# A fused attention and mixture-of-experts block: own lag for every operation, score groups of four lanes, causal mask by GpSimd selects

## The chip, the cores and the metric

The kernel runs on one core of one Trainium2 chip. The metric is the device time of one execution in microseconds (us), as the median of several runs. The core has five engines that each work through a queue of their own, in order: TensorE (PE; its weight loads are listed as PEld), VectorE (DVE), ScalarE (ACT), GpSimd (POOL) and SyncE (SP, here only for DMA). They wait for each other by semaphores.

## The reference

Input x is 8 batches of 256 rows of 128 numbers, all float32. Each batch is normalised (`xn`), and two branches of `xn` are added to x.

```python
x = L0_attn_x
xn = _layernorm(x, axis=-1)
x = x + attn(xn) + ffn(xn)
# attn: qkv = xn @ w_qkv.T; one head, no mask
att = softmax(q @ k.T * 128**-0.5)
y = einsum('bqk,bvd->bqd', att, v) @ w_fc.T + b_fc
return layernorm(xn + y) * gamma + beta
# ffn: 16 heads of 8, causal
h = rms(x, n1_w)
q, k, v = rms(heads(wq), qn_w), rms(heads(wk), kn_w), heads(wv)
scores = where(causal, q @ k.T * 8**-0.5, -inf)
ao = softmax(scores) @ v @ wo.T      # first 32 columns set to 0
x = x + ao
xf = rms(x, n2_w)
wts = top 2 of softmax(xf @ gate_w.T), normalised, over 4 experts
return x + sum(wts[e] * expert_e(xf))   # first 32 columns of the sum are 0
```

The experts are small stacks of 128x256 and 256x256 layers with gelu or silu: `e0` (up, down), `e1` (w1, w2, down, silu by tanh), `e2` (l1, l2, l3, l4), `e3` (down, up, out).

## The kernel before

A batch of 256 rows is two tiles of 128. The work on one batch is cut into four stages, and one slot of the software pipeline works on four batches at a time: L (layer norm, turning `xn`, the projections), A (norm of Q and K by three Newton steps on VectorE, their transposes), B (causal attention, the other attention branch, the output projection, the residual and `xf`) and C (gate and experts). `stages` gives slot t the batches L = t, A = t - 1, B = t - 2, C = t - 3, so 8 batches take 11 slots, t = 0 to 10. All operations of a stage have the same lag. Each engine has a function `slot` in which the order of its operations within a slot is written out by hand, and waits name the exact event that is needed. PSUM has four shared banks (`a`, `pv`, `even`, `odd`), each filled and read in the fixed cyclic order of `BANK_FILLS`, and a four-bank tile `scores_ps`.

Causal attention: the 16 heads stand in 4 lanes of 32 partitions and 4 groups. A matmul of one lane uses 32 rows of the array (`tile_position=(32*lane, 0)`), so lanes can lie side by side in it. `scores(u)` (line 1174) computes one unit, half a group, two lanes: for each lane 256 queries by the first 128 keys and 128 queries by the other 128 keys. There are 8 units for each batch, 64 in all. To each unit's scores TensorE adds the mask (line 1186): a bf16 matmul of the identity with `later_keys`, which holds -1e30 where the key comes after the query. ScalarE's `exp_unit` (line 463) writes exp of a unit to `probs`, unmasked parts and masked ones (which become 0) alike. `weigh_v(g)` (lines 1203 and 1207) multiplies by V with four lanes in four column tiles, and fills bank `pv`; VectorE turns the result (`pv_turn`, line 769). A unit waits only for the exp of the unit two before it, so that two units alternate. A second program, with a search of row maxima (`find_maxima`), runs only if the weights of the norms are large; on these inputs it does not run.

Further names: `x_turn` and `qk_turn` (line 1111) transpose on TensorE; `qkv_project` (1143), `q0_project` (1136), `a0_scores` (1216), `fc_row` (1224); `wo_project` (1232), `xf_turn`, `gate` (1251); `up_layer` (1266) for E1A, E1B, L1, D3, E0; `square_layer` (1278) for L2, L3; `e3_up_layer` (1288) for U3; `down` (1304). ScalarE evacuates with gelu (line 524), tanh (508), copies (484, 491, 500, 536, 538), squares (548). ScalarE has tables for its functions: the order of `slot` puts all exps and the tanh of a slot first and all gelus behind, so a full slot has two switches of table, ACT_TABLE_LOAD. VectorE's pairs of 128x128 operations are `ln_normalise` (975), `h0_norm` (903) and `residual_scale` (945). GpSimd has small powers and 128x256 additions (lines 301 to 417).

```python
# the order of slot on TensorE, one line for each stretch
scores(0); scores(1); a0_scores(0); scores(2); up E1A; scores(3)
a0_scores(1); weigh_v(0); scores(4); up E1B; scores(5); weigh_v(1)
fc_row(); scores(6); scores(7); weigh_v(2); up L1; weigh_v(3); up D3
qk_turn(); L2; U3; L3; wo_project(); up E0
x_turn(); qkv_project(0); down(0); xf_turn(); qkv_project(1)
down(1); q0_project(); gate()
```

Of the kernel before, what the change touches and what calls it, by code (L numbers as in the profile page):

```python
# [1 line left out]

# [2 lines left out]

ALU = mybir.AluOpType
ACT = mybir.ActivationFunctionType
F32 = mybir.dt.float32
F32R = mybir.dt.float32r
# [4 lines left out]
P = 128  # L14
FLOAT_MAX = 3.4028234663852886e38
# [12 lines left out]
}  # L28


def fill_ordinals(slots):

    table = {bank: {} for bank in BANK_FILLS}
    for slot in slots:
        for bank, fills in BANK_FILLS.items():
            for fill, stage in fills:
                if slot[stage] is not None:
                    table[bank][fill, slot[stage]] = len(table[bank])
    return table


def fused_block(nc: bass.Bass, x, cols, rows, w_proj, w_first, w_up, w_mid, w_down, out):
# [14 lines left out]
    with ExitStack() as ctx:  # L57
# [6 lines left out]
        def sem(name):  # L64
# [4 lines left out]
        pv_ps, a_ps = psum("pv_ps"), psum("a_ps")  # L69
        even_ps, odd_ps = psum("even_ps"), psum("odd_ps")  # L70
# [41 lines left out]
        xn = [sb(f"xn{r}", [P, TILES, D]) for r in range(3)]  # L112
# [49 lines left out]
                   ln_stats ln_scaled xn_ready a_full a_read qk_ready v_ready  # L162
                   scores_full exp_done pv_full pv_read
                   a0_maxed a0_rowed xsum_ready h0_stats h0_scaled h0_normed ao_ready
                   xnb_ready x1_started x1_squared x1_scaled xf_ready acc_ready
                   gate_shifted gate_exped e1_tanh
                   even_full even_read odd_full odd_read
                   dve_a dve_b dve_c dve_d dve_l dve_s pool_l pool_b pool_s""".split()
        s = {n: sem(n) for n in names}
# [3 lines left out]
        DVE_A, DVE_B, DVE_C, DVE_D, POOL_L, POOL_B = 14, 4, 15, 6, 5, 3  # L173
# [3 lines left out]
        def stages(t):  # L177
            numbers = {"L": t, "A": t - 1, "B": t - 2, "C": t - 3}
            return {stage: n if 0 <= n < BATCHES else None for stage, n in numbers.items()}

        SLOTS = [stages(t) for t in range(BATCHES + 3)]
        at = fill_ordinals(SLOTS)

        block = ctx.enter_context(nc.Block())

        def wait(eng, name, value):

            if not isinstance(value, int) or value > 0:
                eng.wait_ge(s[name] if isinstance(name, str) else name, value)

        def fill_free(eng, bank, fill, batch):

            wait(eng, f"{bank}_read", at[bank][fill, batch])

        def fill_ready(eng, bank, fill, batch):

            wait(eng, f"{bank}_full", at[bank][fill, batch] + 1)

        def fill_emptied(eng, bank, fill, batch):

            if batch >= 0:
                wait(eng, f"{bank}_read", at[bank][fill, batch] + 1)

        def pipeline(slot):
            for t in range(1, len(SLOTS)):
                slot(**SLOTS[t])


        @block.sync
        def _(sp):  # L210
            sp.dma_start(x_sb[0][:], x[0].rearrange("(j p) d -> p j d", p=P)).then_inc(x_in[0], 16)
            sp.dma_start(proj[:], w_proj).then_inc(s["proj_in"], 16)
            sp.dma_start(first[:], w_first).then_inc(s["first_in"], 16)
            sp.dma_start(x_sb[1][:], x[1].rearrange("(j p) d -> p j d", p=P)).then_inc(x_in[1], 16)
# [4 lines left out]
            def rows_of(t, batch):  # L219
                return t[batch].rearrange("(j p) d -> p j d", p=P)  # L220

            def slot(L, A, B, C):
                if L is not None and L >= 2:
                    wait(sp, "xn_ready", L - 1)
                    sp.dma_start(x_sb[L % 2][:], rows_of(x, L)).then_inc(x_in[L % 2], 16)
                if B is not None:
                    wait(sp, out_done[B % 2], 16 * (B // 2))
                    sp.dma_start(acc[B % 2][:], rows_of(x, B)).then_inc(acc_in[B % 2], 16)
                if C is not None:
                    fill_emptied(sp, "even", "DN0", C)  # L230
                    fill_emptied(sp, "odd", "DN1", C)
                    sp.dma_start(rows_of(out, C), acc[C % 2][:]).then_inc(out_done[C % 2], 16)

            slot(**SLOTS[0])
            pipeline(slot)
# [5 lines left out]
        def _(pool):  # L241
            def step(ins, name, value):

                ins.then_inc(s[name], 1)
                pool.wait_ge(s[name], value)

            step(nc.gpsimd.memset(ident[:], 0.0), "pool_s", 1)
# [4 lines left out]
            def constants():  # L252

                step(nc.gpsimd.memset(lane_rows[:], 1.0), "pool_s", 2)
# [28 lines left out]
                pool.wait_ge(s["zeros_ready"], 2)  # L283

            def slot(L, A, B, C):
                l, a, b = L, A, B
                k = {"pool_l": POOL_L * l if L is not None else 0, "pool_b": POOL_B * b if B is not None else 0}

                def step_of(ins, name):
# [1137 lines left out]
```

## Time and profile before

| what | us |
|---|---|
| median of 3 runs | 306.5 (302.14 to 308.01) |
| the profiled execution | 302.12 |
| its span, first to last instruction | 300.4 |
| TensorE busy | 261.5 |
| ScalarE, VectorE, GpSimd busy | 151.1, 144.5, 73.0 |

The profile is of one execution on the chip. Its page gives the busy time of each engine, the chain of work that ended last, and groups of instructions by line; each further view is an answer of the same trace. Busy time counts overlapping instructions of an engine once. The ends of matmuls are modelled, and spans on GpSimd are rough. Lines such as L1174 are lines of the kernel before.

### The profile page before, as it was taken

What the parts mean: (1) busy time and instruction counts of PE and PEld (TensorE: products, weight loads), DVE (VectorE), ACT (ScalarE), POOL (GpSimd) and SP (SyncE); (2) the same over time, 40 slices, a digit from 0 to 9 for tenths busy, and PEclk for the clock granted to TensorE, in tenths of its full rate; (3) what the DMA queues carried; (4) which work ended last, traced back from release to release, by engine and by line L of the source; (5) the groups of instructions that cost most, each with busy time, mean ns of one, the idle gap of its engine ahead of it and who ended that gap; (6) DMA issues with size and microseconds to landing.
All of it is one profiled execution on the core that took longest, in us unless ns stands there. A gap on an engine that the chain in (4) does not pass through costs nothing.

```text
span 300.4 us, 5450 instructions
## 1 busy us (share of the span) xinstructions
PE 261.5 (87%) x1940; PEld 187.3 (62%) x1940; DVE 144.5 (48%) x608; ACT 151.1 (50%) x298; POOL 73.0 (24%) x163
## 2 busy tenths in 40 slices
PE   0717997599998999899989998999899989998784
PEld 0302654166687667776777676866686678667564
DVE  2360345115742585349522962387248525452713
ACT  1222344334564656556665657556656564654530
POOL 4731301440042223214240515050610052006000
PEclk9999999557999999999999999999999999999999
DMA  7510000000000100010001000010001000000000
GB/s 194 211 39 2 1 0 2 2 0 2 0 0 2 53 2 0 2 52 3 0 3 41 14 0 1 25 30 2 0 3 37 2 0 20 17 2 0 21 0 17
DMA packets 7567, 6.05 MB, mean 20 GB/s; under 512 B 624, under 2 KB 7024, under 8 KB 7536
## 3 DMA queue, kind: packets, MB, share of 16 engines
q1 hardware_dynamic: 7248, 5.44, 5.7%
q10 hardware_dynamic: 288, 0.21, 0.5%
q8 instruction: 18, 0.29, 0.4%
q14 instruction: 13, 0.11, 0.1%
HBM read 4.60 MB, written 1.05 MB: 19 GB/s over the span
## 4 chain that ended last, share of the span: by engine, by line
PE 78%; DVE 6%; DMA 4%; ACT 4%; issue 3%; POOL 1%; SPq 1%; ACTq 0%; DVEq 0%; POOLq 0%
PE scores_ps L1174 17%; PE even_ps L1278 9%; PE scores_ps L1186 6%; PE odd_ps L1266 6%; PE pv_ps L1203 6%; PE a_ps L1143 5%; PE even_ps L1304 5%; PE odd_ps L1304 5%; PE even_ps L1266 4%; PE a_ps L1216 3%; DMA x_sb<-in_x 3%; PE odd_ps L1288 2%; PE pv_ps L1207 2%; PE a_ps L1111 2%; DMA first<-in_first 2%
## 5 line engine op out<-in xcount | busy, mean ns | idle before, releaser
L463 ACT ACTIVATE probs<-scores_ps 128x768 f32<-128x768 f32 x64 | 51.7, 808 | 44.0 <-PE scores_ps L1186 44.0
L1174 PE MATMUL scores_ps<-qT,kT 32*128 32x256 f32 (+1 forms) x512 | 64.4, 373 | 0.0
L1174 PEld LDWEIGHTS scores_ps<-qT,kT 32*128 32x128 f32 x512 | 47.5, 200 | 20.0 <-issue 14.9
L1278 PE MATMUL even_ps<-l_h,mid 128*128 128x256 f32 x128 | 31.0, 385 | 0.0
L327 POOL TENSOR_SCALAR h_rstd<-h_mv 128x2 f32<-128x2 f32 x8 | 1.5, 192 | 113.1 <-DVE h_mv L893 113.1
L1186 PE MATMUL scores_ps<-later_keys,ident_bf 128*128 128x256 bf16 x128 | 26.6, 292 | 0.0
L1143 PE MATMUL a_ps<-qkvT,xnT 128*128 128x384 f32 x32 | 18.4, 663 | 9.4 <-ACT xnT L484 8.0
L1278 PEld LDWEIGHTS even_ps<-l_h,mid 128*128 128x128 f32 x128 | 23.2, 190 | 4.4 <-ACT l_h L524 1.8
L1266 PE MATMUL odd_ps<-xfT,up 128*128 128x256 f32 x80 | 22.3, 394 | 2.3 <-DVE e_h L761 1.7
L769 DVE STREAM_TRANSPOSE pv_rows<-pv_ps 128x256 f32<-128x256 f32 x32 | 14.3, 446 | 19.3 <-PE pv_ps L1207 19.3
L524 ACT ACTIVATE l_h<-even_ps 128x512 f32<-128x512 f32 x24 | 14.6, 607 | 15.9 <-PE even_ps L1278 15.8
L1203 PE MATMUL pv_ps<-probs,v_aug 128*32 128x256 f32 x256 | 20.9, 399 | 0.6 <-DVE pv_rows L769 0.6
L844 DVE TENSOR_REDUCE a_negmax<-a_ps 128x1 f32<-128x256 f32 x16 | 6.6, 414 | 30.3 <-PE a_ps L1216 30.3
L991 DVE SCALAR_TENSOR_TENSOR acc<-even_ps,wts,acc 128x96 f32<-128x96 f32 x32 | 10.2, 318 | 17.5 <-issue 8.5
L1266 PE MATMUL even_ps<-xfT,up 128*128 128x256 f32 x64 | 18.2, 410 | 0.2 <-DVE e_s L752 0.2
L387 POOL TENSOR_SCALAR ln_tmp<-ln_mv 128x2 f32<-128x2 f32 x8 | 2.0, 249 | 63.0 <-DVE ln_mv L964 50.7
L500 ACT ACTIVATE qkv<-a_ps,h_scale 128x384 f32<-128x384 f32 x16 | 9.3, 580 | 15.4 <-PE a_ps L1143 15.4
L945 DVE TENSOR_SCALAR xf<-x_sb,x_scale 128x128 f32<-128x128 f32 x16 | 8.5, 569 | 17.8 <-POOL x_scale L371 17.8
L1266 PEld LDWEIGHTS odd_ps<-xfT,up 128*128 128x128 f32 x80 | 13.4, 190 | 5.4 <-DVE e_h L761 2.1
L1143 PEld LDWEIGHTS a_ps<-qkvT,xnT 128*128 128x128 f32 x32 | 6.1, 236 | 14.1 <-ACT xnT L484 10.4
L473 ACT ACTIVATE a_exp<-a_ps,a_negmax 128x256 f32<-128x256 f32 x16 | 7.6, 474 | 11.6 <-DVE a_negmax L844 11.2
L1266 PEld LDWEIGHTS even_ps<-xfT,up 128*128 128x128 f32 x64 | 11.4, 199 | 3.1 <-issue 1.4
(151 smaller groups left out, 473.7 us busy)
## 6 DMA issues: line engine op xcount, KB each, us to landing
x_sb<-in_x SPq DMA_DIRECT2D x8, 128.0 KB, 2.5
acc<-in_x SPq DMA_DIRECT2D x8, 128.0 KB, 2.1
out<-acc SPq DMA_DIRECT2D x8, 128.0 KB, 1.9
mid<-in_mid SPq DMA_DIRECT2D x1, 640.0 KB, 7.3
up<-in_up SPq DMA_DIRECT2D x1, 578.0 KB, 6.2
downs<-in_down SPq DMA_DIRECT2D x1, 512.0 KB, 8.1
first<-in_first SPq DMA_DIRECT2D x1, 320.0 KB, 5.3
row<-in_rows ACTq DMA_DIRECT2D x1, 200.0 KB, 4.8
```

The lines of the kernel that those rows point to most:

```text
L463: nc.scalar.activation(probs[g % 2][:, 2 * half:2 * half + 2, 0:SEQ + P], scores_ps[:, 2 * half:2 * half + 2, 0:SEQ + P], ACT.Exp).then_in ...
L500: nc.scalar.activation(qkv[:, j, :], a_ps[:, 0:3 * D], ACT.Copy, scale=h_scale[:, j:j + 1]).then_inc(s["a_read"], 1)
L524: nc.scalar.activation(flat, ps[:, 0:ncol], ACT.Gelu).then_inc(s[f"{bank}_read"], 1)
L769: V.transpose(pv_rows[:, g].rearrange("p n e -> p (n e)"), pv_ps[:, 0:SEQ]).then_inc(s["pv_read"], 1)
L991: ins = V.scalar_tensor_tensor(out=rows, in0=(even_ps, odd_ps)[j][:, e * KEPT:(e + 1) * KEPT], scalar=wts[:, j, e:e + 1], in1=rows, op0=AL ...
L1143: T.matmul(a_ps[:, 0:3 * D], xnT[L % 2][:, j * P:(j + 1) * P], qkvT[:], start=True, stop=True).then_inc(s["a_full"], 1)
L1174: ins = T.matmul(ps, kT[p][rows, g, kt * P:(kt + 1) * P], qT[p][rows, kt * P:SEQ], start=kt == 0, stop=False, tile_position=(32 * lane, 0))
L1186: ins = T.matmul(own, ident_bf[:], later_keys[:].unsqueeze(1).to_broadcast([P, TILES, P]), start=False, stop=True)
L1203: T.matmul(rows[:, 0:SEQ], v_aug[p][:, 0, GROUPS * lane + g, :], pr[:, lane, 0:SEQ], start=True, stop=False, tile_position=(0, 32 * lane))
L1266: ins = T.matmul(ps[:, m * SEQ:(m + 1) * SEQ], wT[:, m * P:(m + 1) * P], xfT[C % 2][:], start=True, stop=True)
L1278: ins = T.matmul(even_ps[:, m * SEQ:(m + 1) * SEQ], wT[:, at:at + P], src[:, ci, :], start=(ci == 0), stop=(ci == HC - 1))
L1304: ins = T.matmul(ps[:, e * KEPT:(e + 1) * KEPT], hidden[e][:, ci, j * P:(j + 1) * P], downs[:, e, ci, MASKED:], start=(ci == 0), stop=(ci ...
```

## The change

- Stages are gone. Each operation takes its batch number from the slot with a lag of its own, from 0 to 4, and has a new place in `slot` on its engine. Groups 0 of scores and exps of a batch come one slot before groups 1 to 3; `down` on TensorE comes one slot later than the other expert layers. There are 12 slots, t = 0 to 11.
- The order of the fills of each bank changes with it, and the head (first batch's turn and projections) is written ahead of the slots.
- `scores(n, g)` issues one group, all four lanes, and waits for both exps of the group before.
- The mask matmuls are dropped in the program that runs here. After each exp, GpSimd's `mask(n, u)` sets the part of `probs` with keys behind the query to 0 by an `affine_select` over 128x512 elements, 8 for each batch. `weigh_v` waits for the selects, not for the exps.
- ScalarE's order puts exps between the gelus: L1, E0, L2, D3, then exps of units 0 and 1, then L3, U3, then exps of units 2 and 3.
- Several waits become explicit (what a buffer's reader has done); the two programs remain, with the mask matmuls kept in the one that searches for maxima.

```diff
-    "a": (("S00", "B"), ("S01", "B"), ("FC", "B"), ("QKT", "A"), ("XT", "L"), ("QKV0", "L"), ("QKV1", "L"), ("Q0T", "L")),
+    "a": (("QKV1", 1), ("Q0T", 1), ("S00", 2), ("S01", 2), ("FC", 2), ("QKT", 1), ("XT", 0), ("QKV0", 0)),
...
+            def mask(n, u):
...
+                g, half = divmod(u, HALVES)
+                pool.wait_ge(s["exp_done"], UNITS * n + u + 1)
+                own = probs[g % 2][:, 2 * half:2 * half + 2, :].rearrange("p l (n q) -> p (l n) q", q=SEQ)[:, :, 0:P]
+                nc.gpsimd.affine_select(out=own, in_=own, compare_op=ALU.is_ge, fill=0.0, base=0,
+                                        pattern=[[0, 2 * TILES], [1, P]], channel_multiplier=-1
+                                        ).then_inc(s["masked"], 1)
...
-                    wait(pe, "exp_done", UNITS * b + u - 1)
+                wait(pe, "exp_done", UNITS * n + HALVES * g)
...
-                        for lane in (2 * half, 2 * half + 1):
+                    for lane in range(LANES):
...
-                    wait(pe, "exp_done", UNITS * b + HALVES * (g + 1))
+                wait(pe, "masked", UNITS * n + HALVES * (g + 1))
```

The new orders, as the kernel after has them (lag behind the name):

```python
# TensorE
qkv(1) 1; scores(1) 2; weigh_v(0) 2; q0 1; down(0) 4; down(1) 4; a0_scores(0) 2
xf_turn 3; scores(2) 2; gate 3; E1A 3; a0_scores(1) 2; weigh_v(1) 2
scores(3) 2; E1B 3; fc_row 2; weigh_v(2) 2; L1 3; E0 3; qk_turn 1; L2 3; D3 3
weigh_v(3) 2; x_turn 0; scores(0) 1; qkv(0) 0; L3 3; U3 3; wo 2
# ScalarE
exp 4, 5 of 2; tanh 3; a0_softmax(1) 2; gate_exp 3; exp 6, 7 of 2
gelu L1 3; gelu E0 3; q_copy, k_copy x4 1; gelu L2 3; gelu D3 3; x_copy 0
exp 0 of 1; qkv_copy(0) 0; exp 1 of 1; gelu L3 3; qkv_copy(1) 0; gelu U3 3
x1_square x2 2; exp 2 of 1; q0_copy 0; exp 3 of 1; xf_copy 2; a0_softmax(0) 1
# GpSimd
h0_gamma 3; mask 3 of 2; v_copy 1; h0_beta 3; h0_add 3; mask 4 to 7 of 2
ln x4 0; x1_add 3; h_eps, h_pow 0; biased 1; h0_variance 2; x1_start 2
h0_scale 2; mask 0, 1 of 1; x1_variance, x1_pow 2; mask 2 of 1
```

## Rows read from the trace of the kernel before

**Rows 1.** Page, part 1: busy us (share of the span), instructions

```profile
PE 261.5 (87%) x1940; PEld 187.3 (62%) x1940; DVE 144.5 (48%) x608; ACT 151.1 (50%) x298; POOL 73.0 (24%) x163
```

**Rows 2.** Table by stretch, one full slot: us, length, busy of each engine, clock, DMA

```profile
129.00:160.26 31.26, 29.96 (x243) 22.25 (x242) 17.26 (x75) 18.50 (x38) 8.49 (x17) 1.00 0.05 14
```

**Rows 3.** Chain in order of time, slots at full clock: start us, us, what

```profile
181.27 1.82 PE even_ps L1278 x8
...
186.66 1.76 PE even_ps L1304 x16
...
188.63 0.65 PE a_ps L1143 x2
...
191.84 0.85 PE scores_ps L1174 x8
192.69 0.32 PE scores_ps L1186 x2
...
198.56 0.57 PE pv_ps L1203 x8
199.13 0.22 PE pv_ps L1207 x8
```

**Rows 4.** Page, part 5: group, count, busy us, mean ns, idle before

```profile
L1174 PE MATMUL scores_ps<-qT,kT 32*128 32x256 f32 (+1 forms) x512 | 64.4, 373 | 0.0
L1186 PE MATMUL scores_ps<-later_keys,ident_bf 128*128 128x256 bf16 x128 | 26.6, 292 | 0.0
```

**Rows 5.** Chain in order of time, first 32 us

```profile
16.60 0.59 DVE xn L975 x2
...
19.86 1.10 PE a_ps L1111 x4
...
29.99 1.58 PE scores_ps L1174 x8
```

**Rows 6.** Table by stretch, between the first two attention slots

```profile
50.00:55.00 5.00, 2.34 (x9) 1.70 (x8) 2.26 (x9) 3.01 (x11) 2.45 (x5) 0.64 0.00 0
55.00:60.00 5.00, 2.98 (x6) 0.82 (x4) 0.93 (x2) 1.29 (x3) 2.19 (x4) 0.50 0.01 3
...
65.00:70.00 5.00, 5.00 (x24) 3.42 (x21) 2.53 (x11) 2.09 (x5) 1.93 (x5) 0.50 0.00 0
```

**Rows 7.** Chain in order of time, last 20 us

```profile
280.34 0.98 PE even_ps L1266 x4
...
292.76 2.00 PE even_ps L1304 x16
...
297.70 0.32 DVE acc L991
```

**Rows 8.** Groups by shape, GpSimd

```profile
L357 POOL TENSOR_TENSOR acc<-h0n,acc 128x256 f32<-128x256 f32 x8 | 5.8, 728 | 1.5 <-POOL h0n L349 0.5
...
L277 POOL TENSOR_SCALAR_AFFINE_SELECT mask_f<-mask_f 128x128 f32<-128x128 f32 x2 | 0.6, 298 | 0.3
...
L255 POOL TENSOR_SCALAR_AFFINE_SELECT lane_rows<-lane_rows 128x16 f32<-128x16 f32 x1 | 0.2, 230 | 0.1
```

**Rows 9.** Timeline of weight loads: start us, us, engine, line, tiles, count

```profile
191.77 0.19 PEld L1174 LDWEIGHTS scores_ps<-qT,kT 32*128 32x128 f32 x2
...
198.49 0.16 PEld L1203 LDWEIGHTS pv_ps<-probs,v_aug 128*32 128x32 f32 x8 [0.33 <-issue]
```

**Rows 10.** Timeline of ScalarE at a switch from exp to gelu

```profile
175.01 0.81 ACT L463 ACTIVATE probs<-scores_ps 128x768 f32<-128x768 f32 x1 [0.37 <-PE scores_ps L1186]
175.84 1.28 ACT L524 ACT_TABLE_LOAD   x1
177.14 0.60 ACT L524 ACTIVATE l_h<-even_ps 128x512 f32<-128x512 f32 x1
```

**Rows 11.** Timeline of VectorE and GpSimd, a pair alone and a pair beside GpSimd

```profile
180.24 0.60 DVE L903 TENSOR_SCALAR h0n<-h,h_mv,h_rstd 128x128 f32<-128x128 f32 x2 [0.73 <-POOL h_rstd L334]
...
185.87 0.72 POOL L379 TENSOR_TENSOR acc<-acc,x_sb 128x256 f32<-128x256 f32 x1
...
185.94 0.94 DVE L945 TENSOR_SCALAR xf<-x_sb,x_scale 128x128 f32<-128x128 f32 x2 [2.04 <-POOL x_scale L371]
```

More of the change, by code:

```diff
@@ L14 @@
 P = 128
+XN_COPIES = 3
+SLOTS_AFTER = 4
 FLOAT_MAX = 3.4028234663852886e38
@@ L23, with fill_ordinals, filled @@
 BANK_FILLS = {
[4 rows of a table removed]
-}
[L31 to L38, printed above, removed]
[4 rows of a table added]
+}
+HEAD_FILLS = ("XT", "QKV0", "QKV1", "Q0T")
+BANK_OF = {fill: bank for bank, fills in BANK_FILLS.items() for fill, _ in fills}
+def fill_ordinals(batches, slots):
+    table, count = {}, dict.fromkeys(BANK_FILLS, 0)
+    def filled(fill, batch):
+        if 0 <= batch < batches and (fill, batch) not in table:
+            table[fill, batch] = count[BANK_OF[fill]]
+            count[BANK_OF[fill]] += 1
+    for fill in HEAD_FILLS:
+        filled(fill, 0)
+    for t in range(slots):
+        for fills in BANK_FILLS.values():
+            for fill, lag in fills:
+                filled(fill, t - lag)
     return table
@@ L189, in wait, with fill_free @@
                 eng.wait_ge(s[name] if isinstance(name, str) else name, value)
[L191 to L206, printed above, removed]
+        def fill_free(eng, fill, n):
+            wait(eng, read_sem(fill), at[fill, n])
@@ L217, in _, with load_x, load_acc, store @@
             sp.dma_start(downs[:].rearrange("p e c d -> p (e c d)"), w_down).then_inc(s["down_in"], 16)
[L219 to L235, printed above, removed]
+            def load_x(n):
+                if not 2 <= n < BATCHES:
+                    return
+                wait(sp, "xn_ready", n - 1)
+                sp.dma_start(x_sb[n % 2][:], rows_of(x, n)).then_inc(x_in[n % 2], 16)
+            def load_acc(n):
+                if not live(n):
+                    return
+                wait(sp, out_done[n % 2], 16 * (n // 2))
+                sp.dma_start(acc[n % 2][:], rows_of(x, n)).then_inc(acc_in[n % 2], 16)
+            def store(n):
+                if not live(n):
+                    return
+                fill_emptied(sp, "DN0", n)
+                fill_emptied(sp, "DN1", n)
+                sp.dma_start(rows_of(out, n), acc[n % 2][:]).then_inc(out_done[n % 2], 16)
+            for t in range(BATCHES + 3):
+                load_x(t)
+                load_acc(t - 2)
+                store(t - 3)
             for p in range(2):
@@ L586, in _ @@
-            slot(**SLOTS[0])
-            pipeline(slot)
+            nc.scalar.copy(vfc[:], scores_ps[:, 1, 0:D]).then_inc(s["vfc_ready"], 1)
+            ahead = 1
+            for t in range(SLOTS):
+                slot(t)
         @block.vector
@@ L1184, in scores @@
-                    for lane in (2 * half, 2 * half + 1):
+                            T.matmul(ps, head_rows[rows, g:g + 1].to_broadcast([32, P]), negT[p][rows, kt * P:SEQ],
+                                     start=False, stop=False, tile_position=(32 * lane, 0))
+                    for lane in range(LANES):
                         own = scores_ps[:, lane, :].rearrange("p (n q) -> p n q", q=SEQ)[:, :, 0:P]
@@ new lines, in down @@
+            def down(n, j):
+                if not live(n):
+                    return
+                fill = f"DN{j}"
+                fill_free(pe, fill, n)
+                for done in ("E0", "E1B", "L3", "U3"):
+                    fill_emptied(pe, done, n)
+                if n == 0:
+                    pe.wait_ge(s["down_in"], 16)
+                for e in range(EXPERTS):
+                    for ci in range(HC):
+                        ins = T.matmul(ps_of(fill)[:, e * KEPT:(e + 1) * KEPT], hidden[e][:, ci, j * P:(j + 1) * P],
+                                       downs[:, e, ci, MASKED:], start=(ci == 0), stop=(ci == HC - 1))
+                ins.then_inc(full_sem(fill), 1)
```

1895 lines of the change are left out of this document (974 added, 921 removed), and 6 rows, old and new, of the table BANK_FILLS.

## The prediction, written before the change was run

> **What bounds the kernel now.** I read four views in this order. The page's first part: TensorE is busy for 261.5 of 300.4 us, no other engine for more than half [rows 1]. The table by slot (a slot is one turn of the software pipeline): a full slot takes 31.26 us, with TensorE busy for 29.96, ScalarE 18.50, VectorE 17.26 and GpSimd 8.49 [rows 2]. So in a full slot TensorE idles 1.3 us: its instructions set the pace, and only what leaves its queue counts. The chain in order of time says what fills it: a scores unit (two lanes) takes 0.85 us of tiled matmuls, then 0.32 of mask matmuls over the whole array; PV, with four lanes of the same two widths, takes 0.57 + 0.22 = 0.79 in all [rows 3]. The groups give the totals: 64.4 us for the scores, 26.6 for the masks [rows 4]. Last the ends: attention begins at 29.99, the first full slot ran largely at the lower level of TensorE's clock, and the last slot is a lone chain [rows 5 to 7].
>
> **The masks leave TensorE.** 64 units lose their mask: 26.6 us [rows 4], 8 x 0.32 = 2.6 a slot. GpSimd gets 64 selects of 128x512. No row has that size. Selects of 128x16 take 0.23 and of 128x128 0.30 [rows 8], a slope of 0.6 to 0.7 ns an element, so 0.57 us as the estimate; the nearest dearer row, two inputs of 128x256 in 0.73, scaled to 512 gives 1.45 as upper end; the lower end is 0.30. I take 0.57 (same operation): 4.6 us a slot, GpSimd at 13 of some 26, hidden. But each PV group now waits for exp and then select. Queued behind a waiting select are v_copy, the h0 and x1 chains and the layer norm of the next batch, for which VectorE and then the TensorE transposes wait. At least 2.4 us of other TensorE work lies between a scores group and the PV that needs it, except across a slot's start, so I charge nothing; without that cover it is 0.6 to 1.5 a group.
>
> **Four lanes together.** The first two weight loads of a unit, one for each lane, lie in the same 0.19 us, and in PV all eight weight loads lie within 0.16 us [rows 9]. So row-tiled lanes do run side by side, and 0.85 is the time of one lane's stream and not of two. For four I take 0.85 a group (PV's row, 0.79, is nearest below); if only two run at a time it is 1.70. A full slot falls from 8 x 0.85 = 6.8 to 4 x 0.85 = 3.4, over the run 27 us. What it costs: before, two units alternate, one read by ScalarE while TensorE fills the other; now a group waits until both exps (2 x 0.81) of the last one have read it.
>
> **TensorE's slot** becomes 29.96 - 2.6 - 3.4 = 24.0 us.
>
> **ScalarE gets two more table switches.** Its queue now goes exp, gelu (L1, E0, L2, D3), exp (0, 1), gelu (L3, U3), exp: four switches a slot for two. One costs 1.28 between an exp that ends at 175.82 and a gelu at 177.14, 1.32 in all [rows 10]: + 2.6, ScalarE at 21.1 of 24. The Trainium skill ("ScalarE: Activation LUTs", What ACT_TABLE_LOAD costs) puts a drain of about 1.38 us beside the load, 2.66 for every switch. By that rule four switches would be 10.6 a slot and ScalarE at 26.6, an estimate from that page which would make it the bound. The row leaves no room for a drain there, and the sum goes by the row.
>
> The tightest ring I find runs from the end of scores group 0 to the start of group 2. ScalarE: load 1.3, exp 0.8, qkv copy 0.6, exp 0.8, load 1.3, gelu 0.6, qkv copy 0.6, gelu 0.6, two squares 1.0, load 1.3, exp 0.8, q0 copy 0.4, exp 0.8 = 10.9. TensorE by its chain: two qkv 1.3, L3 1.82, group 1 0.85, PV 0.79, two downs 3.52 [rows 3], and five shorter pieces of 0.22 to 0.86 in the same answer (U3, WO, q0, a0 and the xf transpose), 2.4 together = 10.7. ScalarE's times are those of its groups in the page. So it misses by 0.2. I charge 1.7 us of waits a slot: 1.3 as now, 0.4 for this. Full slot: 24.0 + 1.7 = 25.7.
>
> **Own lags: head.** VectorE's Newton chain loses the 0.6 of the second batch's xn in its middle, so the Q and K transposes start at 19.2 for 19.86 and K is copied by 22.1. The scores of batch 0 no longer queue behind the second batch's projections: they start near 22.8 for 29.99 [rows 5]. There a unit takes 1.58 for 0.85, the lower level of TensorE's clock by its duration. Slot 2's queue at twice the times of rows 3: four groups 6.8, two qkv 3.3, the copy between them 0.6, two PV 2.4, q0 1.2, two a0 1.7, a wait for the softmax 0.9 = 16.9, to 39.7. The rest (fc 0.42, two PV 1.6, transposes 0.66, K's copies 1.2, group 0.85, qkv 0.65, WO 0.42) is 5.8 at the upper level, which TensorE now reaches at 40, and 11 at the lower: slot 3 starts at 45.5 to 51. I take 47, for 62.27 now. Before, TensorE was busy for only 5.3 of the 10 us from 50 to 60, and the granted clock was 0.50 from 55 to 70 [rows 6]; scores units turn to 0.85 only after 71.2, so in 62.27 to 71.2 some 4.5 us are the clock's. The new queue has other work in that gap; I count slot 3 at the upper level, and keep 4.5 for the range.
>
> **Own lags: tail.** One slot more, as the downs are a slot later. Slot 10: downs of batch 6, 3.5, then the last batch's layers, 280.34 to 292.76 now = 12.4, with E0 moved into its gaps, 12.1: 15.6. Slot 11: downs 3.6, VectorE 1.35, store 2.4 = 7.3 [rows 7].
>
> **Sum.** Slot 3 at 47.0; slot 3 without downs 22.2; slots 4 to 7, 4 x 25.7 = 102.8; slot 8 without a new batch 24.8; slot 9, without its first steps (3.3), 22.4; slots 10 and 11 15.6 + 7.3. Span 242.1, from 300.4. The profiled execution took 302.1, 1.7 more than its span: 243.8. The median of the runs shown, 306.5, lies 1.4% above that execution, so I forecast 247 us.
>
> **VectorE and GpSimd.** The same pair of 128x128 VectorE operations takes 0.60 with GpSimd idle and 0.94 while GpSimd adds acc from 185.87 to 186.59 [rows 11]. So GpSimd's reads stop VectorE, and eight selects a slot are eight more such meetings. The Trainium skill ("SBUF — State Buffer", SBUF: two separate sides) says that such an operation and GpSimd's take their common port in turns and the loser fully blocks. By that rule, which the row bears out, the selects could hold VectorE for 8 x 0.57 = 4.6 a slot: 21.9 of 25.7, still below TensorE, but its chains (newton, down, residual) get later. It is a rival.
>
> **The rivals.**
> - *Pairs only* (0.12). Four lanes at once contend, two run at a time: 32 x 0.85 = 27 more, 274. For it: nothing in rows 9 shows four loads of 128 columns together. Against it: the pair's loads overlap fully.
> - *ScalarE's ring sets the slot* (0.12). Its 21.1 busy us can't be packed; both added loads become TensorE waits before the scores: 2.6 x 7.5 slots = 20, 267. For it: the ring above is short by 0.2. Against it: before, scores waited little.
> - *Selects block VectorE* (0.08). Half of the 4.6 us a slot comes through: 8 x 2.3 = 18, 265; all of it, 283.
> - *Slower than before* (0.04): the single hand-over. If the queues never get ahead, TensorE stands before every group for both exps, before PV for a select, and for both added loads: 6.5 + 2.3 + 2.6 = 11.4 a slot, 86 us in 7.5 slots, 333. It decides from 7.5 us of new waits a slot; the saving is 7 a slot with the ends. Against it: 2.4 to 8 us of independent work between groups, and ScalarE has 3 us free.
> - That the change does not do what it says is the first of these; the masks can't stay, as nothing issues them.
>
> **Chances.** Forecast 0.60 (own range 237 to 257: waits of 0.5 to 3 a slot), the rivals as given, 0.02 for less than 235, 0.02 for a hand-over that eats just the gain. The range 232 to 276 holds the lower bounds (groups at 0.79 save 2, no waits at all 13) and the first three rivals; the slow one is left out. A measurement of this kernel tells about 2% from no change: faster by over 2% 0.94, within 0.02, slower 0.04.
>
> **What would show it.** Scores groups of sixteen passes in about 0.85 and none of the mask matmuls: TensorE busy near 205 us. About 31 table loads for 16. Selects near 0.57. First scores near 23, slots of 25 to 26 us, second stretch of low clock gone or short. TensorE waits on exp or on the selects of over 3 us a slot would make the ring or the hand-over right; groups of 1.7 the first rival; VectorE busy over 165 us with the pairs of 0.94 common, the third.

## The result and the profile after

| | before | after |
|---|---|---|
| median, 4 runs each on one chip | 305.75 (302.14 to 308.01) | 236.34 (234.24 to 238.25) |
| profiled execution, its span | 302.12, 300.4 | 236.41, 234.6 |

The ratio is 0.774 (95%: 0.763 to 0.785). Some executions of a kernel take 1.5 to 5% longer than its fastest, and the ratios in this text are worked out without these. The forecast was 247 with a range of 232 to 276: the sign and the range held, the size was 10.7 us too high. The narrower range of 237 to 257, to which the prediction gave its chance of 0.60, was missed by 0.7 us on its low side.

The page of the kernel after, part 1 and three groups of part 5 (before: [rows 1, 4]):

```profile
PE 206.7 (88%) x1812; PEld 156.0 (67%) x1812; DVE 160.5 (68%) x608; ACT 160.3 (68%) x310; POOL 114.1 (49%) x227
...
L324 POOL TENSOR_SCALAR_AFFINE_SELECT probs<-probs 128x512 f32<-128x512 f32 x64 | 40.9, 639 | 48.5 <-ACT probs L506 47.0
...
L1241 PE MATMUL scores_ps<-qT,kT 32*128 32x128 f32 (+1 forms) x512 | 31.4, 361 | 0.3
...
L568 ACT ACT_TABLE_LOAD x14 | 18.0, 1283 | 0.3
```

TensorE has 128 instructions fewer, and the same 512 scores passes take 31.4 us for 64.4. The table by slot (us, length, busy of PE, PEld, DVE, ACT, POOL, granted clock, DMA share, GB/s), from slot 3 to the end:

```profile
43.92:69.39 25.47, 22.84 (x195) 16.51 (x196) 19.40 (x65) 18.48 (x37) 14.76 (x28) 0.93 0.01 2
93.53:117.67 24.14, 24.14 (x227) 18.99 (x227) 19.59 (x75) 20.40 (x40) 13.48 (x25) 1.00 0.06 18
165.93:189.06 23.13, 23.13 (x227) 18.33 (x225) 18.61 (x69) 20.04 (x38) 11.46 (x19) 1.00 0.05 13
189.06:210.24 21.18, 20.82 (x198) 16.56 (x199) 13.20 (x56) 14.11 (x27) 8.64 (x15) 1.00 0.05 14
210.24:227.01 16.77, 13.90 (x77) 11.05 (x77) 8.39 (x38) 7.80 (x15) 3.80 (x6) 1.00 0.03 8
227.01:234.60 7.59, 3.78 (x32) 3.62 (x32) 2.54 (x8) 0.00 (x0) 0.00 (x0) 0.88 0.07 21
```

The second row stands for slots 4 to 7. The reader is to see two equal numbers in it: 24.14 us long, 24.14 busy. TensorE doesn't stop at all; before it was 31.26 with 29.96 busy [rows 2]. Slot 3 is the odd one: 2.6 us idle and a clock of 0.93. The chain in order of time, in a full slot (start, us, what):

```profile
100.71 0.86 PE scores_ps L1241 x16
101.57 0.54 PE pv_ps L1324 x4
```

Sixteen passes, four lanes, take 0.86 where eight took 0.85 and a mask of 0.32 came behind them [rows 3].

### The profile page after: what moved, and what is told of

It is laid out like the page before. It is cut to its first block, busy times and chain, and to the rows that moved or that the text cites. A ratio compares the mean times of both kernels' runs of the same rounds, so it can differ in the third digit from the quotient of the medians.

```text
span 234.6 us, 5596 instructions
## 1 busy us (share of the span) xinstructions
PE 206.7 (88%) x1812; PEld 156.0 (67%) x1812; DVE 160.5 (68%) x608; ACT 160.3 (68%) x310; POOL 114.1 (49%) x227
## 4 chain that ended last, share of the span: by engine, by line
PE 81%; DVE 5%; ACT 4%; issue 3%; POOL 2%; DMA 2%; SPq 0%; POOLq 0%; ACTq 0%; DVEq 0%
PE even_ps L1352 12%; PE scores_ps L1241 12%; PE odd_ps L1338 7%; PE pv_ps L1270 7%; PE even_ps L1338 7%; PE even_ps L1380 6%; PE odd_ps L1380 6%; PE a_ps L1211 6%; PE odd_ps L1364 3%; PE a_ps L1285 3%; PE a_ps L1183 3%; PE pv_ps L1274 3%; DMA first<-in_first 2%; PE pv_ps L1324 2%; PE a_ps L1201 2%
## 5 line engine op out<-in xcount | busy, mean ns | idle before, releaser
L324 POOL TENSOR_SCALAR_AFFINE_SELECT probs<-probs 128x512 f32<-128x512 f32 x64 | 40.9, 639 | 48.5 <-ACT probs L506 47.0
L506 ACT ACTIVATE probs<-scores_ps 128x768 f32<-128x768 f32 x64 | 49.9, 809 | 4.5 <-PE scores_ps L1241 4.4
L1241 PE MATMUL scores_ps<-qT,kT 32*128 32x128 f32 (+1 forms) x512 | 31.4, 361 | 0.3
L1241 PEld LDWEIGHTS scores_ps<-qT,kT 32*128 32x128 f32 x512 | 24.2, 192 | 10.3 <-issue 9.3
L1211 PE MATMUL a_ps<-qkvT,xnT 128*128 128x384 f32 x32 | 17.1, 623 | 2.2 <-ACT qkv L542 1.6
L568 ACT ACT_TABLE_LOAD x14 | 18.0, 1283 | 0.3
L1338 PEld LDWEIGHTS odd_ps<-xfT,up 128*128 128x128 f32 x80 | 14.5, 189 | 3.3 <-DVE acc L1053 1.4
L506 ACT ACT_TABLE_LOAD x12 | 15.4, 1283 | 0.2
L841 DVE TENSOR_TENSOR qk_sq<-qkv 128x512 f32<-128x512 f32 x8 | 5.5, 693 | 13.5 <-ACT qkv L542 13.5
L398 POOL TENSOR_SCALAR x_scale<-x_ms 128x2 f32<-128x2 f32 x8 | 1.5, 193 | 25.7 <-ACT x_sq L599 25.7
L609 ACT ACTIVATE xfT<-pv_ps,col 128x256 f32<-128x256 f32 x8 | 3.8, 474 | 14.0 <-PE pv_ps L1183 14.0
L1338 PEld LDWEIGHTS even_ps<-xfT,up 128*128 128x128 f32 x64 | 11.4, 199 | 2.8 <-issue 1.4
L1274 PE MATMUL pv_ps<-probs,v_aug 128*32 128x128 f32 x256 | 13.1, 277 | 0.0
```

The costliest lines, as they stand in the source:

```text
L324: nc.gpsimd.affine_select(out=own, in_=own, compare_op=ALU.is_ge, fill=0.0, base=0, pattern=[[0, 2 * TILES], [1, P]], channel_multiplier=- ...
L506: nc.scalar.activation(probs[g % 2][:, 2 * half:2 * half + 2, 0:SEQ + P], scores_ps[:, 2 * half:2 * half + 2, 0:SEQ + P], ACT.Exp).then_in ...
L568: nc.scalar.activation(flat, ps_of(fill)[:, 0:ncol], ACT.Gelu).then_inc(read_sem(fill), 1)
L1211: T.matmul(ps_of(fill)[:, 0:3 * D], xnT[n % 2][:, j * P:(j + 1) * P], qkvT[:], start=True, stop=True).then_inc(full_sem(fill), 1)
L1241: ins = T.matmul(ps, kT[p][rows, g, kt * P:(kt + 1) * P], qT[p][rows, kt * P:SEQ], start=kt == 0, stop=kt == 1 and not searching, tile_pos ...
L1274: ins = T.matmul(rows[:, P:SEQ], v_aug[p][:, 1, GROUPS * lane + g, :], pr[:, lane, SEQ:SEQ + P], start=False, stop=True, tile_position=(0, ...
```

## The experiments

There are two kinds: the kernel before with one part of the change (names with b_), and the kernel after with one part undone or moved (names with a_). Each ratio is to executions of the kernel before on the same chip. The median of those that count there is 302.58 us beside b_select, b_four, b_both and a_mask_pe; 302.37 beside a_pairs, a_noswitch, a_noselect and a_double; 305.86 beside b_both_xearly, a_lnfirst and a_xf_early; 302.66 beside a_down_lag. The code cuts show the lines that matter; "..." stands for lines left out.

### One part alone, in the old order

**b_select.** GpSimd's selects in place of the mask matmuls, two-lane units as before.

```diff
+                select(0)
+                select(1)
...
-                    for lane in (2 * half, 2 * half + 1):
+                    for lane in (2 * half, 2 * half + 1) if searching else ():
...
-                    wait(pe, "exp_done", UNITS * b + HALVES * (g + 1))
+                    wait(pe, "masked", UNITS * b + HALVES * (g + 1))
```

> The kernel before with one part of the change alone: the mask matmuls go, GpSimd selects on the exps instead, the order of every other operation stays. My theory (TensorE's queue sets the slot, the selects are covered): each full slot loses the 8 x 0.32 = 2.6 us of masks less some waits before PV of groups 0 and 3, which stand close behind their exps: 31.3 to about 29.3, in all 306 to 289 us. The rival, that a select between exp and PV costs as much as it saves in this order, gives 300 us or more, with TensorE waiting on the selects.

Measured: 295.02 us, ratio 0.972 (0.964 to 0.979). TensorE is busy for 241.0 us of a span of 295.3, where it was 261.5 of 300.4 [rows 1]: 20 us of work gone, 5 of span. A full slot:

```profile
125.49:156.49 31.00, 26.55 (x227) 20.16 (x226) 18.59 (x75) 18.27 (x37) 14.07 (x25) 1.00 0.05 14
```

It has 3.4 us less work than [rows 2] and is 0.3 us shorter, where I had expected 2 us. One of the four full slots ran in part at the lower clock level (15 us of it at a granted clock of 0.66) and took 34.9.

**b_four.** Groups of four lanes, mask matmuls kept.

```diff
-                def scores(u):
+                def scores(g):
...
-                        for lane in (2 * half, 2 * half + 1):
+                        for lane in range(LANES):
```

> The kernel before with another part alone: scores and masks issued as groups of four lanes, each waiting for both exps of the group before; masks still on TensorE, all else in its old order. Theory: a group takes 0.86 for 1.70 and two masks less in switching, 3.4 us less work in a full slot; the old order has only 1.3 to 1.8 us of other work between some groups (1.6 us of exps), so about 1 us a slot comes back as waits on exp: 306 to about 287. Rival (the single hand-over eats the gain): 300 or more.

Measured: 287.17 us (283.07 to 289.15), ratio 0.950 (0.940 to 0.960). A full slot is 30.33 us with TensorE busy for 26.62: 3.3 less work, 0.9 less time. The total met the expected 287, the reason for it didn't: I had expected each full slot to keep 2.4 us of the saving. Of the 19.1 us between the two spans (300.4 and 281.3) the four full slots hold only 3.2. Another 5.0 lie before the first gate product (the matmul `gate`, once a slot: at 61.41 us before, at 56.39 here), 5.9 in the slot behind it, and 4.9 in the last slots. So the number was met by luck.

**b_both.** This has both parts, still with one lag for each stage and the old order.

> The kernel before with both: groups of four lanes and selects by GpSimd, all else in its old order and with its old lags. What is left to the kernel after is then what own lags and places bring. Theory: work of 24.0 us in a full slot as in the kernel after, but waits on exp, on selects and on the batch's chains of 3 to 4 us a slot, and the old head and tail: about 268 us, so that own lags are worth some 30. Rival (the order hardly matters, the work sets the time): 250 or less. Rival (hand-over): over 285.

Measured: 288.10 us, ratio 0.953 (0.945 to 0.961): no better than the lanes alone, and 20 us above what I had expected. The time lies where I had put the rival of the single hand-over (over 285), but the trace does not show that one: in the slot below TensorE waits 1.0 us for exps before its scores. A full slot of it, and three short stretches inside:

```profile
144.64:176.13 31.49, 26.20 (x227) 19.67 (x227) 18.34 (x75) 18.27 (x37) 13.61 (x26) 0.95 0.05 14
154.00:156.00 2.00, 0.61 (x16) 0.41 (x8) 0.43 (x2) 0.00 (x0) 0.33 (x1) 1.00 0.35 101
156.00:158.00 2.00, 0.70 (x2) 0.50 (x2) 1.93 (x9) 1.32 (x4) 1.42 (x3) 0.78 0.11 31
158.00:160.00 2.00, 2.00 (x19) 0.71 (x17) 1.93 (x10) 1.87 (x5) 1.75 (x5) 0.50 0.00 0
```

TensorE's busy time fell from 29.96 to 26.20, at a clock of 0.95, and the slot is as long as ever. (The 14.8 us by which the span is shorter lie elsewhere: 5.3 before the first gate product, 5.4 in the slot behind it, 6.6 in the two slots without a new batch, while the four full slots together are 2.6 longer.) What took the place of the work is in the timeline, and a wait of 2.18 to 2.68 us stands there in each of the four full slots:

```profile
157.30 1.22 PE L1233 MATMUL a_ps<-xnT,q0T 128*128 128x256 f32 x2 [2.68 <-ACT a_exp L491]
158.44 1.08 PE L1220 MATMUL pv_ps<-probs,v_aug 128*32 128x256 f32 x8
```

The a0 softmax is late because VectorE's maximum for it stands in its queue behind the LayerNorm statistics, and these wait for x. The chain shows why x is late: SyncE's load (2.82 us in the chain) stands in its queue behind the store of the slot before, which waits for VectorE's last `down`. Around this wait the granted clock goes from 1.00 to 0.50, and the first part of PV takes 1.08, as against 0.64 in the same view at the upper level. So I had two candidates for the loss: this one ring, or the order as a whole.

**b_both_xearly** breaks the ring, and only that.

```diff
-                if L is not None and L >= 2:
-                    wait(sp, "xn_ready", L - 1)
-                    sp.dma_start(x_sb[L % 2][:], rows_of(x, L)).then_inc(x_in[L % 2], 16)
+                if L is not None and 2 <= L + 1 < BATCHES:
+                    wait(sp, "xn_ready", L)
+                    sp.dma_start(x_sb[(L + 1) % 2][:], rows_of(x, L + 1)).then_inc(x_in[(L + 1) % 2], 16)
```

> The kernel before with both parts (b_both), and one thing more: SyncE issues the load of batch L+1's x at the top of a slot instead of loading batch L's x there, behind the store of the slot before. Theory (the ring down -> acc -> store -> load of x -> LayerNorm statistics, with the softmax of a0 queued behind them on VectorE, and then a low clock, is what gave the saved work back): the 2.7 us wait of TensorE before the a0 scores goes, the full slot falls from 31.5 to some 28, with the granted clock in it near 1.00, and the kernel comes to some 262 us. Rival (the old order as a whole is too tight, each wait hides another of the same size): the slot stays at 30.5 or more, 280 us or more.

Measured: 283.95 us, ratio 0.930 (0.922 to 0.938). The wait before a0 is gone, and the slot is 31.21 us:

```profile
118.86:150.07 31.21, 26.16 (x228) 19.57 (x227) 20.22 (x75) 18.22 (x37) 13.56 (x25) 0.95 0.05 14
```

```profile
128.17 0.64 PE L1220 MATMUL pv_ps<-probs,v_aug 128*32 128x256 f32 x8 [1.12 <-DVE pv_rows L787]
...
132.52 0.93 PE L1220 MATMUL pv_ps<-probs,v_aug 128*32 128x256 f32 x8 [2.21 <-DVE pv_rows L787]
```

PV now waits for VectorE to turn the PV before it, which stands in VectorE's queue among the Newton steps. 3.3 us of such waits replaced the 2.7 before a0, with a drop of clock behind them as before (0.67 from 131 to 136). The theory of one ring fell; the rival stood: take one wait away and the next one of its size is there.

### One part undone, in the new order

**a_mask_pe.** The mask matmuls return behind each group, the selects go, and PV waits for the exps.

```diff
+                for lane in range(LANES):
+                    own = scores_ps[:, lane, :].rearrange("p (n q) -> p n q", q=SEQ)[:, :, 0:P]
+                    ins = T.matmul(own, ident_bf[:], later_keys[:].unsqueeze(1).to_broadcast([P, TILES, P]), ...)
...
-                wait(pe, "masked", UNITS * n + HALVES * (g + 1))
+                wait(pe, "exp_done", UNITS * n + HALVES * (g + 1))
```

> The kernel after with the mask matmuls back on TensorE (four behind each group) and no selects; PV waits for the exps. Theory: its full slots are wholly TensorE work (24.13 of 24.13), so the slot grows by the masks' full 4 x 0.6 to 0.65 = 2.5 us, 8 batches 20 us, less about 2 us in the first slots where selects stand in the way: 236 to about 254. If the selects cost something in the full slots the gain is less than that: under 248.

Measured: 248.04 us, ratio 0.818 (0.814 to 0.823). The slot:

```profile
70.47:96.16 25.69, 25.69 (x245) 20.24 (x244) 18.91 (x75) 20.59 (x40) 8.05 (x17) 1.00 0.06 17
```

The slot is 1.55 us longer than in the kernel after. So sixteen masks in four stretches cost that much, and neither the 2.6 of eight stretches by [rows 3] nor the 2.5 I had expected; this is the main reason why the kernel is 6 us faster than its forecast. TensorE never stops in either slot, so in a full slot the masks cost just TensorE's time, and the selects cost it next to nothing.

**a_pairs.** The passes of a group in the old order, first two lanes, then the other two.

```diff
-                for kt in range(TILES):
-                    for lane in range(LANES):
+                for kt, lane in [(kt, 2 * half + i) for half in range(HALVES) for kt in range(TILES) for i in range(2)]:
```

> The kernel after with the 16 matmul passes of a scores group in another order: lanes 0 and 1 for both widths, then lanes 2 and 3, same instructions, same waits. Theory (lanes run side by side only if they follow each other in the queue): a group takes 1.70 for 0.86, 32 x 0.84 = 27 us more, 236 to 262, all of it in TensorE's busy time. Rival (what counts is that no mask matmul of the whole array stands between the pairs, and later passes overtake): a group of 1.1 or less, under 245.

Measured: 237.00 us, ratio 0.782 (0.777 to 0.788), and groups of 0.88 in the chain. So the order inside a group hardly matters. The trace of b_select says the same of the old units. Where two of them came right behind one another with no mask between them, its chain and timeline have

```profile
249.53 0.88 PE scores_ps L1192 x16
```

```profile
249.46 0.95 PE L1192 MATMUL scores_ps<-qT,kT 32*128 32x256 f32 x16
250.34 0.70 PE L1234 MATMUL a_ps<-xnT,q0T 128*128 128x256 f32 x2
251.29 0.92 PE L1192 MATMUL scores_ps<-qT,kT 32*128 32x256 f32 x8 [0.25 <-ACT probs L481]
```

In the second view sixteen passes take 0.95 and eight take 0.92 (the first view counts the same sixteen as 0.88). So four lanes run side by side whenever sixteen passes stand together. What kept the two units of the kernel before apart was the full-array matmul between them: a mask, or a0 or an expert layer. Whether a tiled matmul between them would do the same, no run shows.

**a_noswitch.** Gelu is replaced by Tanh, which lies in the table of exp; this kernel computes another function.

```diff
-                nc.scalar.activation(flat, ps_of(fill)[:, 0:ncol], ACT.Gelu)...
+                nc.scalar.activation(flat, ps_of(fill)[:, 0:ncol], ACT.Tanh)...
```

> The kernel after with Tanh in the place of Gelu (another function of the experts is computed), which needs no switch of table beside Exp: the 26 table loads, 33 us of ScalarE, go to one or two. Theory (TensorE's queue is never kept waiting in the full slots): slots 4 to 8 stay at 24.1 and ScalarE's busy time falls from 20.4 to about 15.3 in them; only first and last slots gain, 1.3 to 3 us in all: 234. The ring rival of the prediction (the added loads pace the slots): 220 or less.

Measured: 235.64 us, ratio 0.780 (0.777 to 0.783), with ScalarE busy for 126.8 us instead of 160.3 and a full slot of 24.10. 33 us less of ScalarE's time changed the median by 0.7 us, which is less than the spread of the executions (235.25 to 237.09 here, 234.24 to 238.25 for the kernel after).

**a_noselect.** The selects are left out, so the causal mask is not applied. **a_double** does each of them twice.

```diff
 # a_noselect
-                wait(pe, "masked", UNITS * n + HALVES * (g + 1))
+                wait(pe, "exp_done", UNITS * n + HALVES * (g + 1))
 # a_double
+                then(nc.gpsimd.affine_select(out=own, in_=own, ...), ("first", u), n)
+                need(("first", u), n)
```

> The kernel after without the selects: the causal mask is left out of the computation, PV waits for the exps. Theory: nothing in the full slots (24.1), VectorE's busy time there back from 19.6 to about 17.3, since GpSimd no longer stops it; in slots 2 and 3, which run by the latency of VectorE's queue, 2 to 3 us less: 234. Rival (selects delay PV in full slots): 230 or less.

> The kernel after with every select issued twice, one behind the other (the second changes nothing): 64 more of 0.64 us on GpSimd, 5.1 us a full slot, GpSimd's busy time 13.4 to 18.5 of 24.1. Theory: the cover is used up; VectorE is stopped by another 2 us a slot and PV waits 0.6 later where the selects stand close before it: slots of 25 to 26, 245 us. If the cover were wide the slots would stay at 24.1 (238); if GpSimd's queue became the bound, 27 and more (260).

Measured: 234.00 us, ratio 0.774 (0.772 to 0.776), with VectorE busy for 153.6 us (160.5 with the selects) and the full slots at 24.10; and 245.04 us, ratio 0.811 (0.807 to 0.814), with VectorE at 172.1. A slot of a_noselect and one of a_double:

```profile
76.08:100.18 24.10, 24.10 (x230) 18.99 (x227) 18.87 (x77) 20.51 (x41) 8.05 (x17) 1.00 0.06 18
73.26:98.29 25.03, 24.44 (x228) 18.82 (x227) 20.63 (x75) 20.49 (x40) 18.73 (x34) 1.00 0.06 18
```

The selects do hold VectorE, 7 us in the run and 0.7 in a full slot. I had expected 2.3 there: without them VectorE is still busy for 18.87, and not for the 17.26 of [rows 2], so most of its growth has another cause. Only outside the full slots does TensorE see any of it, 1.3 us up to the gate product of slot 3. Twice as many selects make a slot 0.9 us longer: TensorE waits 0.6 for VectorE's late `down`, and in no full slot for a select. Another 4.0 of the 8.5 us that the span grew lie before the gate product of slot 3.

**a_lnfirst.** VectorE's LayerNorm statistics go back to the front of its slot, before E1's product.

```diff
+                ln_statistics(t)
+                ln_moments(t)
                 e1_product(t - 3)
                 qk_norm(t - 1)
                 h0_sum(t - 2)
-                ln_statistics(t)
-                ln_moments(t)
```

> The kernel after with one place changed: VectorE's LayerNorm statistics of the next batch stand first in its slot, as they did before, ahead of E1's product, the Q and K norm and h0. Theory (the place of an operation that waits for a DMA sets who waits with it): VectorE stops some 2 us at it in each slot, the Q and K norm comes later, and the transposes, K's copies and the next batch's first scores behind it; 0.5 to 1.5 us a full slot, 238 to 243 us. Rival (there is slack enough between the norm and its transposes): no change, 235 to 237 us.

Measured: 248.09 us, ratio 0.811 (0.801 to 0.821): 12 us for the place of two small steps. A slot, VectorE's wait, and TensorE's:

```profile
98.10:123.74 25.64, 24.61 (x229) 18.82 (x227) 19.73 (x75) 20.50 (x40) 13.18 (x25) 1.00 0.06 17
```

```profile
112.65 0.48 DVE L1017 BATCH_NORM_STATS2 ln_st<-x_sb 128x6 f32<-128x128 f32 x2 [0.92 <-DMA x_sb<-in_x]
```

```profile
114.10 1.13 PE L1338 MATMUL odd_ps<-xfT,up 128*128 128x256 f32 x4 [1.03 <-DVE e_h L825]
```

VectorE waits for x, and E1's product, queued behind, empties its bank late. I had expected the Q and K norm to be the victim and at most 1.5 us a slot. Three things add up to the 11.4 us of span: two full slots grew by 1.5 each, the two behind them by 2.2 and 2.9 (there the wait is 1.74 and 2.43 us), and slots 2 and 3 by 3.3 together.

**a_down_lag.** The downs of a batch go back into the slot of its expert layers, and the order of the bank fills with them.

```diff
-                down(t - 4, 0)
-                down(t - 4, 1)
...
                 wo_project(t - 2)
+                down(t - 3, 0)
+                down(t - 3, 1)
 # ScalarE
-                qkv_copy(t, 1)
                 gelu(t - 3, "U3", u3_h, ("DN0", "DN1"))
+                qkv_copy(t, 1)
```

> The kernel after with the lag of one pair of operations taken back: TensorE's two down projections of a batch stand again at the end of the slot of their expert layers, behind WO (as in the kernel before, where all of stage C had one lag), instead of five operations later in the next slot; ScalarE's gelu of U3 moves ahead of the copy of QKV1, which would otherwise wait for it. In the kernel after, U3 is full at 92.96, its gelu ends at 95.5 behind that of L3 (a table load in front of it, 92.64 to 93.93) and a copy, and the downs start at 96.3, behind 3.0 us of other work. Theory (each lag puts enough of TensorE's other work between a producer's chain and its reader): with the copy out of the way the gelu ends near 95.0, TensorE stands idle from 93.4 until then, 1.6 us in each of the slots with experts, and the kernel comes to some 249 us (246 to 254), a full slot to 25.7. Rival (the clock falls in these gaps, or VectorE's and SyncE's chains behind the downs knock on): 256 us or more. Other rival (one lag is worth nothing by itself): 238 or less.

Measured: 267.22 us, ratio 0.880 (0.872 to 0.888). One pair of operations with its old lag and place costs 31 us, of the 69 that the change brings. A slot, a stretch of it, and TensorE's waits in it (us in total, times, longest):

```profile
105.12:135.13 30.01, 26.34 (x228) 20.61 (x227) 19.66 (x75) 20.48 (x39) 13.28 (x25) 0.94 0.05 14
...
131.00:135.13 4.13, 4.13 (x24) 4.13 (x24) 0.00 (x0) 0.00 (x0) 0.00 (x0) 0.59 0.00 0
```

```profile
PE even_ps L1380 <- ACT u_h L568: 1.6, 1, 1.6
PE a_ps L1285 <- ACT q0T L533: 1.6, 1, 1.6
PE odd_ps L1338 <- DVE acc L1053: 0.4, 1, 0.4
```

The first wait listed, before the downs, is the expected 1.6. The second is the knock-on: while TensorE does the downs, QKV1 isn't issued, ScalarE stands idle for 4.64 us before its copy, and its squares, table load and exp then delay the copy of q0. And behind the wait before the downs the clock falls to 0.59 of full, so the downs themselves are slow. This does not happen each time: behind the same wait of 1.63 us the downs take 3.62 us at 101.50, with the granted clock at 1.00, and 5.24 at 129.89. From gate product to gate product the slot with the first is 28.4 us long and the one with the second 30.0, so of the 5.9 us that such a slot grew the clock has 1.6, and the two waits with what follows from them the rest. The rival with the falling clock and the knock-on won.

**a_xf_early**, an attempt at a better kernel. In slot 3 of the kernel after TensorE waits for xf (timelines of TensorE, GpSimd and VectorE):

```profile
50.45 0.41 PE L1183 MATMUL pv_ps<-ident,xf 128*128 128x128 f32 x2 [2.17 <-DVE xf L1008]
```

```profile
46.62 0.69 POOL L404 TENSOR_TENSOR x_scale<-x_scale,minus_half 128x2 f32<-128x2 f32 x1
47.27 0.64 POOL L324 TENSOR_SCALAR_AFFINE_SELECT probs<-probs 128x512 f32<-128x512 f32 x1
```

```profile
47.44 0.52 DVE L860 TENSOR_SCALAR qk_t<-qk_ms 128x64 int32<-128x64 int32 x1
47.98 0.66 DVE L867 TENSOR_SCALAR qk_y<-qk_t 128x64 int32<-128x64 int32 x1
48.68 0.58 DVE L875 TENSOR_TENSOR qk_t<-qk_y 128x64 f32<-128x64 f32 x1
49.18 1.12 DVE L1008 TENSOR_SCALAR xf<-x_sb,x_scale 128x128 f32<-128x128 f32 x2
```

The factor is there at 47.31, and xf starts 1.87 us later, behind three small steps that take 0.20 to 0.23 in a full slot and 0.52 to 0.66 here, beside GpSimd. The selects are not the main cause: in a_noselect, which has none, the three steps take 0.62, 0.30 and 0.68 beside GpSimd's h0 operations, TensorE still waits 1.84 us for xf, and the clock from 50 to 55 is 0.66.

```diff
                 rsqrt_input(t)
+                residual_scale(t - 2)
                 rsqrt_halve(t)
                 rsqrt_guess(t)
                 newton_square(t, 0)
-                residual_scale(t - 2)
```

> The kernel after with one place changed: VectorE's scaling of xf stands right behind the first step of the inverse square root instead of four small steps later. In slot 3 it stood from 47.31, when its factor was ready, to 49.18 behind four steps that are stretched beside GpSimd's selects, and TensorE was idle for 2.17 us before the transposes of xf, with a granted clock of 0.69 in the 5 us behind. Theory: TensorE's idle time there falls by 1.5 us or more, the low clock behind it goes or shrinks, and the kernel gains 1.5 to 3 us, 233.5 to 235 us; the full slots stay at 24.1. Rival (another input of TensorE, or the clock's history, comes next there): within 0.5 us of the kernel after.

Measured: 231.51 us (231.16 to 233.68, 6 runs), ratio 0.761 (0.755 to 0.767). Slot 3, from its first projection:

```profile
41.81:63.99 22.18, 21.12 (x194) 15.29 (x195) 18.93 (x65) 18.12 (x37) 15.23 (x28) 1.00 0.01 2
```

The gain is 4.8 us where I had expected 1.5 to 3. Slot 3 fell from 25.47 to 22.18 us: 1.6 of it is the wait, most of the rest the clock, which is 1.00 throughout and was 0.69 from 50 to 55. Full slots stay at 24.13. The profiled execution also began slot 3 2.1 us earlier, because the clock had risen in slot 2 some 4 us sooner; nothing in this edit reaches there, so 3.3 us are the edit's and 2.1 are not shown to be. The interval of its ratio overlaps that of the kernel after (0.763 to 0.785); each of the six times is below its lowest, 234.24.

## Why the prediction was right, and where it was off

The span came out at 234.6 for 242.1. By its own terms, forecast and measured: start of slot 3 47.0 and 43.92; slot 3 22.2 and 25.47; slots 4 to 7 102.8 and 96.54; slot 8 24.8 and 23.13; slot 9 22.4 and 21.18; slots 10 and 11 22.9 and 24.36. The differences, -3.1, +3.3, -6.3, -1.7, -1.2 and +1.5, make the 7.5. The other 3 us are the factor of 1.4% from one execution to the median: here the median is the profiled execution. That factor was carried over from the kernel before and had no reason of its own.

- **Masks leave TensorE, selects at 0.57.** The selects take 0.64, well inside the bounds, and no PV waits for one in a full slot. The cover of 2.4 us was real: even with twice as many selects (a_double) no PV in a full slot waits for one. What a_double uses up is VectorE's slack.
- **Four lanes in 0.85.** Measured 0.86; "pairs only" fell. The reading "the time of one lane's stream and not of two" gave the right number. It didn't say why two units took twice as long: a_pairs and b_select show that it is what stands between them.
- **TensorE's slot of 24.0.** Measured 24.14. The two cuts together held to 0.1; taken one by one they don't add so neatly, since the mask alone is worth 1.55 in the new order (a_mask_pe) and not 2.6.
- **"I charge 1.7 us of waits a slot": the step that failed.** Measured: none in the full slots. That is 6.3 us in slots 4 to 7 and most of 2.9 in slots 8 and 9. The ring was taken as 10.9 on ScalarE for 10.7 on TensorE. ScalarE's side in a full slot, its first and its last step:

```profile
89.34 1.28 ACT L506 ACT_TABLE_LOAD   x1
...
98.57 0.83 ACT L506 ACTIVATE probs<-scores_ps 128x768 f32<-128x768 f32 x1
```

  Group 0 ends at 89.61, and the table load started before that, so the load isn't wholly in the ring; the last exp ends at 99.40, 9.8 us later, and TensorE takes up group 2 at 100.64. TensorE's side takes 11.0 where the sum had 10.7, ScalarE's 9.8 where it had 10.9. The ring has 1.2 us to spare. I also carried over the 1.3 of idle time "as now", though the waits behind it belonged to the old order.
- **Two more table switches.** The loads go from 16 to 28 (forecast: about 31), 1283 ns each, and ScalarE's slot is 20.40 for 21.1. Its ring as a rival fell with a_noswitch. By the price of a switch in the Trainium skill ("ScalarE: Activation LUTs", What ACT_TABLE_LOAD costs) the prediction's estimate had ScalarE at 26.6 in a slot; the slot is 24.14 with ScalarE idle for 3.7 of it, so the trace does not agree and the row was right.
- **Selects block VectorE.** This is real, small and hidden. VectorE's slot grew from 17.26 to 19.59, which looks like the half of 4.6 that the rival named. But a_noselect has 18.87 and a_mask_pe 18.91 without any select, so the selects account for 0.7 of it; the other 1.6 came with the new order, and no run shows more closely from what. The slack of 4.6 us took both. The Trainium skill's rule of the common port ("SBUF — State Buffer", SBUF: two separate sides) agrees with this trace: the pair that took 0.60 alone takes 1.23 beside two selects at 44.16. The time paid for it lies before slot 3 (1.0 us) and in slot 3 (0.3), by a_noselect.
- **Head.** First scores at 23.04 for 22.8. TensorE reached its upper clock level near 31 and not near 40 (in the timeline groups take 1.67 up to 28.46 and 0.94 from 33.43), hence slot 3 at 43.92.
- **Slot 3 at the upper level, 22.2.** It met a wait of 2.17 us and a clock of 0.69 behind it. With a wait of 0.54 and the clock at 1.00 it is 22.18 (a_xf_early), the forecast's number.
- **What the sum didn't say.** It took the cut work straight off the slot, as if that needed nothing, and gave the own lags credit for head and tail alone. b_both shows that in the old order a full slot gets no shorter by the cuts: 31.49 for 31.26. Both cuts without the lags are worth some 15 us (0.953), where the prediction has 26.6 for the masks and 27 for the lanes. The lags and places bring the other 50 or so, and taking back one pair of downs costs 31. So it was partly luck that the sum came near: cuts and lags came together, and the term for waits, which was wrong, was small.

These points are left open: which of the other lags and places matter (only three were undone), why the clock rises at different times in slot 2 of two nearly equal kernels, and why it falls behind some waits and not behind others of the same length.

## What to carry to other kernels

Work cut from the engine that bounds a pipeline shortens a slot only if the waits don't grow; so look first for what each in-order queue puts between a producer's chain and its reader, in the new order, and price the cut by that. An operation that waits for another engine should have independent work ahead of it in its queue (the downs of the kernel after have 3.0 us of it), which one lag more gave here for a longer tail (24.36 us in slots 10 and 11). And an idle gap on TensorE costs more than itself where the clock falls behind it: 5.24 us for the downs that take 3.62 at the upper level.

## What was not expected of the hardware

- Row-tiled passes of four lanes overlap in both orders that were run (16 in 0.86 and in 0.88 us), and a matmul over the whole array between two lots of eight makes them 0.85 each.
- A wait of 2.68 us (b_both) or 1.63 us (a_down_lag, at 129.89) was followed by a granted clock of 0.50 to 0.59, that is near the 1.2 GHz level, for some 4 us. The length of the wait alone doesn't decide it: behind the 1.63 us at 101.50 in a_down_lag, behind 1.87 us in a slot of b_four and behind 2.43 us in a_lnfirst the granted clock stayed at 1.00.
- In the first 31 us the granted clock in the profile reads 1.00 while scores groups take 1.59 us and not 0.86: there only the durations show the lower level.
- GpSimd's work stretches single VectorE operations to two or three times their length where they meet. Beside selects of 128x512, operations of 0.21 and 0.22 us take 0.63 and 0.66 (kernel after, at 102.61 and 103.27). Beside its 128x256 operations, with no select in the kernel, one of 0.20 takes 0.62 (a_noselect, at 46.46).
